# Cross attentions: exponentials over two score banks, the fp32 one in SBUF, and scores four units ahead

## The reference

```
x = x + xattn0(ctx, layernorm(x), ...)
x = x + attn0(...) ; x = x + ffn0(...)
x = x + xattn1(ctx, layernorm(x), mask, ...)
x = x + attn1(...) ; x = x + ffn1(...)

def xattn(x, latents, [mask], Wq, Wkv, Wo, ...):          # 16 heads of 64
    xn, ln = layernorm(x) * w1 + b1, layernorm(latents) * w2 + b2
    q = ln @ Wq
    k, v = split(concat([xn, ln], axis=1) @ Wkv)
    logits = einsum('bhld,bhsd->bhls', q, k) / sqrt(64)    # masked in the second
    return einsum('bhls,bhsd->bhld', softmax(logits), v) @ Wo
```

## Time and profile before

| | us |
|---|---|
| median of 3 runs | 2077.18 (2076.81 to 2078.1) |
| span of the profiled execution | 2072.1 |
| PE busy, share of the span | 1926.2, 93% |
| DVE busy | 1681.9, 81% |
| ACT busy | 1237.5, 60% |
| POOL busy | 833.8, 40% |
| granted TensorE clock, mean | 0.976 |

### The profile page before, as it was taken

The page is one execution under the profiler, slowest core; times in us unless marked ns, Lnnn a source line. Parts: engine busy times, 40 slices in busy tenths (PEclk is TensorE's granted clock), DMA queues, the critical chain, the costliest instruction groups (busy, mean ns, idle before and its releaser), DMA issues. The chain is left out here.

```text
span 2072.1 us, 34571 instructions
## 1 busy us (share of the span) xinstructions
PE 1926.2 (93%) x12154; PEld 1046.0 (50%) x12154; DVE 1681.9 (81%) x3998; ACT 1237.5 (60%) x2218; POOL 833.8 (40%) x911
## 2 busy tenths in 40 slices
PE   6899999999999999888898999999999999998886
PEld 6444544445454544533757445454545454544584
DVE  6799889889989896699566788879797978885657
ACT  4366666665757666444224776867777777766312
POOL 5576565666666651098001424333232323231000
PEclk9899999999999999999998999999999999999997
DMA  4332322222222220132104011111121111110000
GB/s 138 89 99 65 75 67 67 67 68 67 75 71 67 51 67 1 47 113 90 40 0 126 14 38 46 43 38 39 38 60 38 39 38 42 34 30 9 21 1 10
DMA packets 148837, 110.51 MB, mean 53 GB/s; under 512 B 120876, under 2 KB 136216, under 8 KB 148664
## 3 DMA queue, kind: packets, MB, share of 16 engines
q1 hardware_dynamic: 148664, 108.31, 18.9%
HBM read 65.15 MB, written 14.29 MB: 38 GB/s over the span
## 5 line engine op out<-in xcount | busy, mean ns | idle before, releaser
L1256 DVE TENSOR_TENSOR x_p_lo<-x_psum,x_p_hi 128x512 f16<-128x512 f32 (+1 forms) x864 | 583.9, 682 | 112.7 <-ACT x_psum L1023 111.8
L1022 ACT ACTIVATE x_p_hi<-x_psum 128x512 f16<-128x512 f32 (+1 forms) x448 | 268.1, 599 | 260.8 <-PE x_psum L857 211.2
L1022 ACT ACTIVATE x_p_hi<-x_psum,x_bcol 128x512 f16<-128x512 f32 (+1 forms) x416 | 289.6, 696 | 153.8 <-PE x_psum L857 151.8
L883 PE MATMUL x_psum<-x_p_hi,x_x_both 128*128 128x512 f16 (+1 forms) x832 | 316.7, 381 | 30.3 <-DVE x_p_lo L1256 29.4
L855 PE MATMUL x_psum<-x_q,x_xT_both 128*128 128x512 f16 x832 | 316.8, 381 | 5.6 <-DMA x_q<-x_shift_rows 5.5
L856 PE MATMUL x_psum<-x_q,x_xT_both 128*128 128x512 f16 x832 | 315.8, 380 | 0.0
L857 PE MATMUL x_psum<-x_q,x_xT_both 128*128 128x512 f16 x832 | 315.8, 380 | 0.0
L885 PE MATMUL x_psum<-x_p_hi,x_x_both 128*128 128x512 f16 (+1 forms) x832 | 315.3, 379 | 0.0
L884 PE MATMUL x_psum<-x_p_lo,x_x_both 128*128 128x512 f16 (+1 forms) x832 | 315.3, 379 | 0.0
L1195 DVE CUSTOM_DVE_ANT_0 x_junk<-x_psum,x_brow 128x512 bf16<-128x512 f32 (+2 forms) x512 | 279.3, 584 | 9.1 <-PE x_psum L941 7.2
L1198 DVE TENSOR_REDUCE x_mx<-x_psum 128x1 f32<-128x512 f32 (+2 forms) x512 | 276.6, 583 | 2.5 <-PE x_psum L941 1.5
(11 more groups left out here) (469 smaller groups left out, 3488.1 us busy)
## 6 DMA issues: line engine op xcount, KB each, us to landing
x_x_both<-context_rows SPq DMA_DIRECT2D x32, 832.0 KB, 5.1
context_rows<-x_x SPq DMA_DIRECT2D x16, 832.0 KB, 3.5
x_raw<-in_ctx SPq DMA_DIRECT2D x16, 768.0 KB
ssm_c_row<-ssm_bc_rows SPq DMA_DIRECT2D x16, 512.0 KB, 4.2
ssm_b_wide<-ssm_bc_rows SPq DMA_DIRECT2D x7, 512.0 KB, 3.5
x_mrow<-in_mask_BxS_bk SPq DMA_DIRECT2D x16, 200.1 KB
x_Wkv<-in_L_xattn_Wkv SPq DMA_DIRECT2D x4, 512.0 KB, 5.2
x_xT_both<-context_rows SPq DMA_TRANSPOSE x96, 3.9
```

The lines of the kernel that those rows point to most:

```text
L883: pe.matmul(out, v_hi, p_hi[r][rows, :], start=start, stop=False)
L1022: act.activation(p_hi[r][rows, :], score[r][rows, :], ACT.Exp, scale=SCORE_UNIT, **bias).then_inc(p_hi_ready, 1)
L1256: v.tensor_tensor(p_lo[r][rows, :], score[r][rows, :], p_hi[r][rows, :], ALU.subtract).then_inc(p_lo_ready, 1)
```

## The change

- ACT works by tiles: its two exponentials cover both units of a tile (1024 columns, two PSUM banks). The fp32 one goes to an SBUF tile `p32` (two of them in turn) and no longer back to PSUM. The f16 tiles `p_hi` and `p_lo` are 1024 wide, three in turn.
- DVE takes the difference of a whole tile, from `p32` and `p_hi`, both in SBUF; the first tile of a body is cut into its two units.
- PE issues the scores of unit u+4 in step u. A score slot is two banks, and is free when the tile's fp32 exponential is done, not when the difference is.
- The first scores of the next body are issued from step 24 (even) or 25 (odd) on.
- The order in which items are read follows from two new functions. DVE reads max, turn and out items of steps 2j-3 and 2j-2 ahead of the difference of tile j; it reads q items of step 1 behind tile 2's difference, of steps 2 and 3 behind tile 3's, of step 4 behind tile 4's. ACT reads the same q items behind the exponentials of tiles 2, 3 and 4. In odd bodies the max items now are two to a step in steps 6 and 7, and the turn stands in step 20 instead of 22; even bodies keep theirs.
- ACT copies the sums of a body out behind the first exponentials of the next one.
- The split sums share the memory of `vo_c` and `vo_l`, which are no longer needed by then.
- At the end, ACT and DVE split the last sums into f16 parts, and the last outputs go through the same f16 matmuls as the others.

The diff, cut to its core:

```diff
-        vo_c, vo_l = sb("vo_c", [P, H, D + 1]), sb("vo_l", [P, H, D + 1])
+        vo_both = sb("vo_both", [P, 2, H * (D + 1)])
...
-    RING = 4
-    p_hi = [sb(f"p_hi{k}", [P, HALF], F16) for k in range(RING)]
-    p_lo = [sb(f"p_lo{k}", [P, HALF], F16) for k in range(RING)]
+    SLOTS, P_RING, WIDE_RING = 2, 3, 2
+    p_hi = [sb(f"p_hi{k}", [P, HL], F16) for k in range(P_RING)]
+    p_lo = [sb(f"p_lo{k}", [P, HL], F16) for k in range(P_RING)]
+    p32 = [sb(f"p32_{k}", [P, HL]) for k in range(WIDE_RING)]
...
-    LAG = 1
     LAST = STEPS - 1
-    AHEAD = 3
-    HOLD = 2
-    TURN_BY = LAST - 4
+    TILES = KT + 1
+    AHEAD = 2 * SLOTS
+    HOLD = (1, 2)
+    XT_AFTER = 6
+    TURN_BY = LAST - 6
...
+    def read_by_vector(items):
+        at, out = 0, {}
+        for u in sorted(items):
+            for item in items[u]:
+                if item[0] != "lat":
+                    at = max(at, 2 * ((u + 4) // 2) + 1 if item[0] == "q" else 2 * ((u + 3) // 2))
+                    out.setdefault(min(at, 2 * KT + 1), []).append(item)
+        return out
+
+    def read_by_scalar(items, j):
+        return [item for u in (2 * j - 4, 2 * j - 3) for item in items.get(u, []) if item[0] == "q"]
...
 (SP)
-                    wait_alone(sp, s_ready, at.half + 2 * AHEAD)
+                    wait_alone(sp, s_ready, at.half + XT_AFTER)
...
 (PE, scores)
-                if not (isinstance(half, int) and half + user_before(u) < 0):
-                    pe.wait_ge(p_lo_ready, half + user_before(u) + 1)
+                if u % 2 == 0 and b * TILES + j >= SLOTS:
+                    pe.wait_ge(p32_ready, b * TILES + j - SLOTS + 1)
...
 (PE, body)
-                    elif at.has_next and u > LAST - AHEAD + HOLD:
+                    elif at.has_next and u + AHEAD - STEPS >= HOLD[at.par]:
                         k = u + AHEAD - STEPS
-                        for k in range(0 if k == HOLD else k, k + 1):
+                        for k in range(0 if k == HOLD[at.par] else k, k + 1):
                             scores(k, at.npar, at.half + STEPS, at.n, at.ni)
...
 (PE, end)
-            pe.wait_ge(sum_out, B)
-            pe.wait_ge(sum_out1, B)
-            pe.wait_ge(aux_free, 2 * k)
+            pe.wait_ge(sum_parted, 2 * (B - 1))
             for a in range(OUT_ITEMS):
-                last_outputs(a, last_place(a)).then_inc(aux_ready, 2)
+                pe.wait_ge(last_low, 3 if a == 0 else 4)
+                outputs(a, last_place(a)).then_inc(aux_ready, 2)
...
 (ACT, probabilities of tile j)
-                act.activation(p_hi[r][rows, :], score[r][rows, :], ACT.Exp, scale=SCORE_UNIT, **bias).then_inc(p_hi_ready, 1)
-                act.activation(score[r][rows, :], score[r][rows, :], ACT.Exp, scale=SCORE_UNIT, **bias).then_inc(p32_ready, 1)
+                act.wait_ge(s_ready, units_done(at.b, j))
+                if g >= P_RING:
+                    act.wait_ge(pv_done, units_done(at.b, j - P_RING))
+                if g >= WIDE_RING:
+                    act.wait_ge(p_lo_ready, units_done(at.b, j - WIDE_RING))
+                src = score_slot[j % SLOTS][rows, cols]
+                act.activation(p_hi[g % P_RING][rows, cols], src, ACT.Exp, scale=SCORE_UNIT, **bias)
+                act.activation(p32[g % WIDE_RING][rows, cols], src, ACT.Exp, scale=SCORE_UNIT, **bias).then_inc(p32_ready, 1)
...
 (ACT, body)
-                for u in range(STEPS):
-                    probabilities(u, at)
-                    for item in at.items.get(u - LAG, []):
+                for j in range(TILES):
+                    probabilities(j, at)
+                    if j == 0 and at.b:
+                        context_sums(at.b - 1, 1 - at.par)
+                    for item in read_by_scalar(at.items, j):
                         parts(at, item)
...
 (DVE, body)
+                for j in range(TILES):
+                    g = at.b * TILES + j
+                    rows = slice(0, TAIL if j == CT else P)
+                    read_items(2 * j)
+                    v.wait_ge(p32_ready, g + 1)
+                    cuts = (0, HALF, HL) if j == 0 else (0, HL) if j < KT else (0, HALF)
+                    for start, end in zip(cuts, cuts[1:]):
+                        lo, whole, hi = (x[rows, start:end] for x in (p_lo[g % P_RING], p32[g % WIDE_RING], p_hi[g % P_RING]))
+                        v.tensor_tensor(lo, whole, hi, ALU.subtract).then_inc(p_lo_ready, (end - start) // HALF)
+                    if j == 0 and at.b:
+                        latents_sums(at.half, 1 - at.par)
+                    for u in (2 * j, 2 * j + 1):
...                     (statistics as before)
+                    read_items(2 * j + 1)
...
 (DVE, end)
+            for k, (part, src, hs) in enumerate(LAST_SUMS):
+                hi, lo = (x[:, hs, 1, :] for x in sum16[part])
+                v.wait_ge(last_high, k + 1)
+                v.tensor_tensor(lo, src, hi, ALU.subtract).then_inc(last_low, 1)
```

More of the change, by code:

```diff
@@ L882, in products @@
                     pe.wait_ge(sum_out1, at.b)
-                pe.matmul(out, v_hi, p_hi[r][rows, :], start=start, stop=False)
-                pe.matmul(out, v_hi, p_lo[r][rows, :], start=False, stop=False)
-                pe.matmul(out, v_lo, p_hi[r][rows, :], start=False, stop=stop).then_inc(pv_done, 1)
+                pe.matmul(out, v_hi, p_hi[r][rows, mine], start=start, stop=False)
+                pe.matmul(out, v_hi, p_lo[r][rows, mine], start=False, stop=False)
+                pe.matmul(out, v_lo, p_hi[r][rows, mine], start=False, stop=stop).then_inc(pv_done, 1)
             def outputs(a, at):
@@ L1030, in body @@
             def body(at):
-                for u in range(STEPS):
-                    probabilities(u, at)
-                    for item in at.items.get(u - LAG, []):
+                for j in range(TILES):
[3 more added lines that the diff above has]
+                    for item in read_by_scalar(at.items, j):
                         parts(at, item)
-                if not at.first:
-                    wait_alone(act, sum_parted, 2 * (at.b - 1))
-                act.wait_ge(pv_done, at.half + 2 * KT - 1)
-                act.activation(sum_c[:, 0:8, at.par, :], acc[0].rearrange("p (h l) -> p h l", l=L), ACT.Copy).then_inc(sum_out, 1)
             every(act, before, body)
+            for k, (part, src, hs) in enumerate(LAST_SUMS):
+                act.wait_ge(pv_done, B * STEPS - (2, 1, 0, 0)[k])
+                act.activation(sum16[part][0][:, hs, 1, :], src, ACT.Copy).then_inc(last_high, 1)
         @block.gpsimd
@@ L1139, in body @@
                     if masked:
-                        mask_col(at.n, at.npar, at.ni, None if at.first and at.par == 0 else at.half - (STEPS - 2 * KT))
+                        mask_col(at.n, at.npar, at.ni, None if at.first and at.par == 0 else (at.b - 1) * TILES + KT)
                     if at.par == 0:
@@ L1251, in body, with read_items @@
             def body(at):
-                for u in range(STEPS):
-                    j, r = u // 2, u % RING
-                    rows = slice(0, TAIL if j == CT else P)
-                    v.wait_ge(p32_ready, at.half + u + 1)
-                    v.tensor_tensor(p_lo[r][rows, :], score[r][rows, :], p_hi[r][rows, :], ALU.subtract).then_inc(p_lo_ready, 1)
-                    if u == 1 and not (at.first and at.par == 0):
-                        latents_sums(at.half, 1 - at.par)
-                    two, three = stats_parts(u, at) if not masked else ((), ())
-                    for part in two if at.has_next2 else ():
-                        context_stats(v, wait_alone, at.b + 2, at.par, at.i + 1, part)
-                    for part in three if at.has_next3 else ():
-                        context_stats(v, wait_alone, at.b + 3, at.npar, at.ni + 1, part)
-                    for item in at.items.get(u - LAG, []):
+                def read_items(place):
+                    for item in at.by_vector.get(place, []):
                         if item[0] == "out":
@@ L1268, in body @@
                             consume(at, item)
-                if not at.first:
-                    wait_alone(v, sum_parted, 2 * (at.b - 1))
-                v.wait_ge(pv_done, at.half + 2 * KT)
-                v.tensor_copy(sum_c[:, 8:16, at.par, :], acc[1].rearrange("p (h l) -> p h l", l=L)).then_inc(sum_out1, 1)
+                for j in range(TILES):
+                    g = at.b * TILES + j
+                    rows = slice(0, TAIL if j == CT else P)
[8 more added lines that the diff above has]
+                    for u in (2 * j, 2 * j + 1):
+                        two, three = stats_parts(u, at) if not masked else ((), ())
+                        for part in two if at.has_next2 else ():
+                            context_stats(v, wait_alone, at.b + 2, at.par, at.i + 1, part)
+                        for part in three if at.has_next3 else ():
+                            context_stats(v, wait_alone, at.b + 3, at.npar, at.ni + 1, part)
```

(11 more changed lines are left out.)

61 lines of the change are left out of this document (33 added, 28 removed).

## The result

The changed kernel takes 2427.6 us (2426.0 to 2430.9), the kernel before in the same runs 2077.0: a ratio of 1.17, 95% interval 1.1686 to 1.1714. That is 350 us slower, where 178 were forecast, and above the range's upper end of 2330. The direction was right, but the forecast was half of the loss.

A forecast was written before the change was run, and what follows sets the result against it. PE was taken as the bound, DVE close behind in x0. Span 2072.1 + 74 (hand-over) + 83 (POOL) + 25 (seams) - 3.6 (end) = 2250.5; with 5.1 added, rounded down, 2255 us, range 2110 to 2330.

The forecast's parts named there:

- The hand-over: Odd bodies: PE's q items and first max item wait until ACT and DVE have read q; +74 us.
- PE has P(1), q, S(6) and P(2), 3.26: 0.6: q of step 2 waits behind tile 2 for q of step 1; PE's own work of 3.26 us leaves 0.6 us stall.
- today's stalls: Stalls of 0.68 and some 0.2 us at the q items before, taken off 6.2 us per odd body, leaving +5.3.
- Differences against POOL: DVE's wide differences, both inputs in SBUF, wait for POOL's instruction to end: +83 us, bounds 0 and 119.
- at random: Differences assumed to meet POOL's long instructions at random: 9.1 us of waiting per pair in x0, 6.7 in x1.
- the factor: Share of the differences' waiting for POOL taken to reach PE uncovered: 0.7, bounds 0 and 1.
- POOL waits as much, but is idle 37 us of a pair in x0, and nobody waits for it sooner: POOL's own waiting beside the differences was given no cost.
- Max items, seams, end: Max, turn, out items and seams between bodies: 1.8 us per pair, +25 us; end of both attentions: -3.6 us.
- the 1.8 forecast: End of each attention: 64 f32 matmuls of 7.2 us become 96 f16 ones of 5.4 us, -1.8 us each.
- the hand-over alone: Rival: wide differences seldom meet POOL, or another wait covers theirs; 2172 us, range 2103 to 2220, chance 0.28.
- a gain: Rival: ACT reaches q early enough, PE never waits, today's stalls go; 2017 us, with half 2047; chance 0.06.
- the third rival: DVE becomes the bound: waits uncovered, wide operations a fifth slower, seams at upper bound; 2330 us; above 2330 chance 0.07.

The follow-up runs named there:

- experiment 10: Changed kernel, DVE reading the items behind a tile's difference ahead of the statistics of that tile's units: 2417.5 us.
- Experiment 2: Changed kernel with matmuls of no use in place of PE's longest waits, no wait removed: 2387.0 us.
- experiment 3: Kernel before with only the fp32 exponential of 512 columns sent to SBUF instead of PSUM: 2243.0 us.
- Experiment 4: Changed kernel, from the third pair on POOL's casts, two-input operations and mask rows cut to one or a few columns: 2311.0 us.

## Why the prediction was wrong in size

*The hand-over: mechanism right, 74 forecast, 112 measured (71.7 ahead of q items, 39.8 ahead of the first max item).* The third q item and the first max item came out near what was worked out (3.2 and 2.5 forecast; 2.6 to 3.4, once 5.3, and 2.6 to 3.3 measured). The step that failed is "PE has P(1), q, S(6) and P(2), 3.26: 0.6": the statistics of x0 are counted nowhere in it, although in the code they stand between the difference and the read, and the wait was 3.3 us. In six pairs of x0 that is 16 of the missing 38 us; experiment 10 puts 1.9 of the 2.7 us in each down to the statistics, the rest stays open. Some 8 more are a matter of the account: of the 0.9 us per pair that were taken off as today's stalls most stood ahead of a product, where the table has them. What remains is spread over waits of 0.5 us at the first q item, the first max item and the third q item of x1.

*The clock: nothing forecast, 79 us.* This is the largest failed step, and it is a step that is missing: the stalls of "about 3 and 2.5 us" were priced at their own length. The two pairs that the forecast read stand at 1.00. But the trace of before has the half clock too (its mean is 0.976), and it has waits of 3 us and more. Behind the 5.49 us that the first score of x0 waits for a DMA the granted clock is half; behind the one wait of 3 us inside the loop it is full:

```profile
74.11:77.08 2.97, 2.97 (x8) 1.05 (x9) 0.35 (x1) 1.28 (x3) 0.00 (x0) 0.50 0.00 0
115.78 0.39 PE L883 MATMUL x_psum<-x_p_hi,x_x_both 128*128 128x512 f16 x1 [3.15 <-DVE x_p_lo L1256]
115.78:119.50 3.72, 3.72 (x20) 1.48 (x21) 3.72 (x13) 1.86 (x4) 3.58 (x2) 1.00 0.36 85
```

So the rows of before left it open what a wait of 3 us brings. The forecast created such waits, and should have given the half clock a price or a rival, for instance the items behind each wait at twice their time. Experiment 2 shows the cause.

*Differences against POOL: mechanism right, 83 forecast, about 117 measured at the products.* The wide differences took 142 us more than their shortest form in both loops, 66 in x0 and 76 in x1, where 9.1 and 6.7 us per pair over 7.5 pairs, 118 in all, were worked out from meetings at random, and 0.7 of it was taken. Two steps failed. One is the factor: 0.82, 117 of 142, came out on PE's path. The other is "at random": in x0 the sum came out as forecast (66 for 68), in x1, forecast as the lighter case, it was half as large again (76 for 50). The meetings are not at random: in three successive pairs of x0 the lengthened differences start 27, 32, 35, 58 and 60 us into the pair each time. That x0 came out right by a random count is therefore luck. Experiments 3 and 4 show the cause from both sides. Experiment 4 also takes 117 us off, but that is another sum, with the half clock and the out items in it; that POOL is nearly the whole rise at the products rests on its 3.5 and 4.1 us per pair.

*"POOL waits as much, but is idle 37 us of a pair in x0, and nobody waits for it sooner": wrong, 15 us.* In the kernel before the last half of the sums ends 1.57 us ahead of the first out item (494.14 + 2.13 against 497.84):

```profile
474.21 10.42 POOL L292 TENSOR_SCALAR x_xt<-x_raw,x_xmean,x_xr 128x127 f32<-128x127 f32 x13
...
494.14 2.13 POOL L1046 TENSOR_TENSOR x_sum_llo<-x_sum_l,x_sum_lhi 128x1024 f16<-128x1024 f32 x1
...
497.84 0.22 PE L893 MATMUL x_psum<-x_vo_chi,x_sum_chi 128*128 128x129 f16 x1
```

After the change POOL's 13 scalings take 14.8 us instead of 10.4 and its casts up to twice their time, and PE waits 2.4 us for POOL in six pairs of x0. Idle time of an engine over a pair says nothing on the slack at the one place where it is awaited.

*Max items, seams, end.* 25 forecast; 25 at max items and 10 for the rest were measured. No run took these apart, so why they came out larger stays open. In x0, from the last product to the next stage's first operation it is 12.81 us instead of 14.55, 1.74 less: the 1.8 forecast holds.

Of the rivals, the hand-over alone (2172) is refuted by experiments 3 and 4, a gain by the rows. DVE did not become the bound: it is busy for 74% of the span (81% before). The 2330 of the third rival was too low: its parts left out the clock.

The account adds up: 38 us from the hand-over, 79 from the clock, 34 from the differences, 10 from max items and seams, 15 from the out items, 176 in all; the span of 2426.2 is 175.7 above the 2250.5 of the forecast's sum.

## What to carry to other kernels

An operand moved from PSUM to SBUF is not free for DVE when GpSimd works beside it (166 us in experiment 3): look for two-input DVE operations that already meet GpSimd in the trace, and count meetings at their fixed places, on both engines. The waits of about 3 us that this change put on PE cost more than their length, by the half clock behind them; where such a wait can't be removed, matmuls in it can pay, as experiment 2 shows. Before operations are widened to gain slack, see what DVE has queued ahead of the late one: moving two groups of DVE's operations behind a difference gained 21 us where the change lost 350.

## What the runs showed of the hardware

The meetings of DVE and POOL are not symmetric for every form. A wide difference ran in 1.23 us inside POOL's run of 128x127 scalings (518.87, the scalings from 512.91 to 523.99), and so did all 35 that began inside one, none of them above 1.29 us, while the thirteen scalings of another body took 14.76 instead of 10.42 us beside differences. POOL's two-input operations and the uint8 mask row held DVE up (603.62 and 1681.58 above). The Trainium skill (SBUF — State Buffer, section "SBUF: two separate sides") gives the port pair to whichever starts first, for its whole instruction; the trace agrees for the mask row, a one-input operation too (the difference of 65 rows that began under it took 2.71 us instead of 1.21; the row of 3.31 us at 1681.58 holds a short one behind it as well), not for these scalings.

Work that nobody reads can make a kernel faster: 39 matmuls in each of seven pairs of x0 and 25 in seven of x1 took 41 us off the time, by the granted clock.
